# Expert rows of a mixture layer: weighted before they are stored, and gathered with an add into the residual

## The reference, cut to what matters

```
x = x + L0_attn(layernorm(x)); x = x + L0_xattn(layernorm(x), ctx)
x = x + L0_ffn(layernorm(x))     # 8 experts, 2 of them per token
x = x + L1_attn(layernorm(x))    # time mix (a scan over 256 tokens), then channel mix
x = x + L1_xattn(layernorm(x), ctx, bias); x = x + L1_ffn(layernorm(x))

# L0_ffn
probs = softmax(xt @ gate_w.T); top_w, top_i = top_k(probs, 2)
top_w = top_w / (sum(top_w) + 1e-9)
h   = gelu(xt @ w1[e] + b1[e]);  out_all = h @ w2[e] + b2[e]
out = sum_k top_w[k] * out_all[top_i[k]]
```

## Time and profile before

| | |
|---|---|
| median of 3 runs | 2008.58 us (2007.64 to 2011.26) |
| the profiled execution | 2000.81 us, its span 1999.0 us |
| PE busy | 1697.9 us, 85% of the span |
| DVE busy | 1245.6 us, 62% |
| ACT busy | 1120.9 us, 56% |
| POOL busy | 561.1 us, 28% |
| mean granted TensorE clock | 0.947 |

### The profile page before, as it was taken

The page is one execution under the profiler, slowest core; times in us unless marked ns, Lnnn a source line. Parts: engine busy times, 40 slices in busy tenths (PEclk is TensorE's granted clock), DMA queues, the critical chain, the costliest instruction groups (busy, mean ns, idle before and its releaser), DMA issues. The chain is left out here.

```text
span 1999.0 us, 40906 instructions
## 1 busy us (share of the span) xinstructions
PE 1697.9 (85%) x13535; PEld 1402.2 (70%) x13540; DVE 1245.6 (62%) x4276; ACT 1120.9 (56%) x2552; POOL 561.1 (28%) x719
## 2 busy tenths in 40 slices
PE   6677777774899999999956999999978999999963
PEld 5455555553688888889945777777866888888842
DVE  6689999868211111111118999998837988888756
ACT  2399999930222222223325666666627888888855
POOL 3333232330211111101025666666520000000017
PEclk9899999987899999999977999999999999999985
DMA  3100000025455555548930000000010000000002
GB/s 116 46 26 22 22 25 18 2 78 183 137 178 192 176 193 175 195 163 280 324 114 18 15 20 22 22 22 22 11 40 12 23 23 23 23 23 23 2 1 85
DMA packets 102048, 154.67 MB, mean 77 GB/s; under 512 B 5760, under 2 KB 85504, under 8 KB 101088
## 3 DMA queue, kind: packets, MB, share of 16 engines
q1 hardware_dynamic: 85600, 125.25, 19.1%
q0 software_dynamic: 6480, 17.70, 3.0%
q10 hardware_dynamic: 9776, 9.31, 1.3%
HBM read 134.54 MB, written 17.69 MB: 76 GB/s over the span
## 5 line engine op out<-in xcount | busy, mean ns | idle before, releaser
L1870 ACT ACTIVATE moe_hT<-moe_p_h,lane_a 128x256 f32<-128x256 f32 (+1 forms) x344 | 131.3, 433 | 370.1 <-PE moe_p_h L1822 370.1
L1822 PE MATMUL moe_p_h<-moe_gT,moe_w 128*128 128x256 f32 (+1 forms) x1376 | 255.8, 344 | 0.8 <-issue 0.8
L1832 PE MATMUL moe_p_y<-moe_w,moe_hT 128*128 128x256 f32 x1136 | 252.3, 379 | 0.0
L1822 PEld LDWEIGHTS moe_p_h<-moe_gT,moe_w 128*128 128x128 f32 x1376 | 227.4, 192 | 25.6 <-issue 1.2
L1362 ACT ACTIVATE xb_pr<-xb_sc,xb_nmax 128x256 f32<-128x256 f32 x512 | 225.3, 502 | 16.7 <-DVE xb_nmax L1441 16.5
L1832 PEld LDWEIGHTS moe_p_y<-moe_w,moe_hT 128*128 128x128 f32 x1136 | 212.6, 190 | 27.0
L1441 DVE CUSTOM_DVE_ANT_0 xb_sc<-xb_p_s,xb_neg 128x256 f32<-128x256 f32 x512 | 187.0, 419 | 55.1 <-PE xb_p_s L1204 46.2
L852 ACT ACTIVATE xa_pr<-xa_sc,xa_nmax 128x256 f32<-128x256 f32 (+1 forms) x512 | 204.6, 456 | 3.4 <-DVE xa_nmax L934 2.9
L1739 POOL DMA_INDIRECT moe_gx<-moe_tokens,moe_source_i x71 | 67.3, 947 | 456.5 <-PE moe_p_t L1809 400.4
L1990 DVE COPY moe_gT<-moe_p_t 128x512 f32<-128x512 f32 (+1 forms) x43 | 25.7, 598 | 232.0 <-PE moe_p_t L1809 232.0
L2015 DVE TENSOR_TENSOR moe_gy<-moe_p_y,lane_a 128x256 f32<-128x256 f32 x71 | 27.5, 420 | 229.1 <-PE moe_p_y L1832 229.1
(11 more groups left out here) (337 smaller groups left out, 3429.7 us busy)
## 6 DMA issues: line engine op xcount, KB each, us to landing
moe_w<-in_L_ffn_w_dram SPq DMA_DIRECT2D x86, 1024.0 KB, 8.1
moe_rows_out<-moe_gy ACTq DMA_DIRECT2D x28, 256.0 KB, 7.1
X<-in_x_dram SPq DMA_DIRECT2D x4, 1024.0 KB, 9.6
xa_ctx<-in_ctx_dram SPq DMA_DIRECT2D x16, 256.0 KB, 2.9
...
```

What stands on the lines that cost most here:

```text
L1822: last = pe.matmul(p_h[n % 3][:, k * width:(k + 1) * width], w1[:, r, ic, (2 * n + k) * P:(2 * n + k + 1) * P], gT[:, r % 2, ic, 0:width], ...
L1832: last = pe.matmul(p_y[:, t * D:(t + 1) * D], hT[:, hc, t * P:(t + 1) * P], w2[:, r, hc, :], start=(hc == 0), stop=(hc == HC - 1))
L1870: last = act.activation(hT[:, 2 * n + k, 0:width], p_h[n % 3][:, k * width:(k + 1) * width], ACT.Gelu, bias=b1[:, bass.ds(e * HC + 2 * n + ...
```

## The change

Three things change. (1) DVE works out `wt` before it waits for `counted`, and ACT's queue stores the 8192 weights, four bytes each, to a new array `weights` in memory. Token numbers in the table are shifted so that none is zero, and the one-hot products of the first and the second choice go to separate columns of `p_y`; from both DVE makes `source_i` as before and `weight_i`, the place of each slot's weight in `weights`. (2) POOL gathers each slot's weight behind the token rows of its group (71 more indirect gathers, of 128 single floats), DVE scales `b2` by it into `b2_w`, and `gy` becomes `p_y * weight + b2_w`, so that the rows in `rows_out` are weighted. (3) In the mix phase `which`, `got` and `combine` are gone: POOL gathers from `rows_out` straight into `X` with an add done by the DMA, indexed by `place_i`. The first choices of batch b + 5 and the second choices of batch b + 4 are issued in turn b; a second choice waits until the first choice of the same batch has landed. `measure_x(n)` waits for the second choice of batch n.

```diff
 # moe, POOL: token numbers without zero
+            chain.done(pool.tensor_scalar(token_up[:, :], token[:, :], 0.0, None, ALU.is_ge))
+            chain.wait()
+            chain.done(pool.tensor_tensor(token[:, :], token[:, :], token_up[:, :], ALU.add))
+            chain.wait()
...
+            def draw_weights(j):
+                if j >= RING:
+                    pool.wait_ge(s_["gy_ready"], j - RING + 1)
+                for t in range(tiles(j)):
+                    n = first_row(j) // P + t
+                    pool.indirect_dma_start(weight[:, j % RING, t:t + 1], None, weights,
+                                            bass.IndirectOffsetOnAxis(ap=weight_i[:, n:n + 1], axis=0)).then_inc(weighed[j % RING], 16)
...
+                if j == RING - 1:
+                    pool.wait_ge(s_["places_ready"], 1)
+                    pool.wait_ge(s_["loaded_back"], 16)
+                    for i in range(RING):
+                        draw_weights(i)
+                elif j >= RING:
+                    draw_weights(j)
 # moe, PE: one-hot products by choice
-                    last = pe.matmul(p_y[:, 0:NBLK], at_row[:, g % 4, n, :], at_blk[:, g % 4, n, :],
-                                     start=(g == 0 and n == 0), stop=(8 * g + n == 2 * NT - 1))
+                    k, at = divmod(8 * g + n, NT)
+                    last = pe.matmul(p_y[:, k * NBLK:(k + 1) * NBLK], at_row[:, g % 4, n, :], at_blk[:, g % 4, n, :],
+                                     start=(at == 0), stop=(at == NT - 1))
 # moe, ACT
+            act.wait_ge(s_["weights_ready"], 1)
+                act.dma_start(weights.rearrange("(k t p) a -> p (k t a)", k=2, p=P), wt[:, :, :].rearrange("p k t -> p (k t)")).then_inc(s_["loaded_back"], 16)
 # moe, DVE: behind gap_ready, ahead of counted (the same eight steps are taken out behind read_rows(0, 0))
+            dve.wait_ge(s_["exp_ready"], 1)
+            step(dve.tensor_reduce(zsum[:, :], probs[:, :, :], AX.X, ALU.add))
...
+            dve.sem_inc(s_["weights_ready"], 1)
 # moe, DVE: the inverse tables
-            dve.tensor_scalar(source_i[:, :], p_y[:, 0:NBLK], float(MID), None, ALU.add).then_inc(s_["source_ready"], 1)
+            step(dve.tensor_copy(codes[:, :, :], p_y[:, 0:2 * NBLK].rearrange("p (k n) -> p k n", k=2)))
+            step(dve.tensor_tensor(code[:, :], codes[:, 0, :], codes[:, 1, :], ALU.add))
+            step(dve.tensor_scalar(code_up[:, :], code[:, :], 0.0, -1.0, ALU.is_gt, ALU.mult))
+            step(dve.scalar_tensor_tensor(source[:, :], code[:, :], float(MID), code_up[:, :], ALU.add, ALU.add))
+            dve.tensor_copy(source_i[:, :], source[:, :]).then_inc(s_["source_ready"], 1)
+            step(dve.tensor_scalar(code_up[:, :], codes[:, 1, :], 0.0, float(B * S), ALU.not_equal, ALU.mult))
+            dve.tensor_tensor(weight_i[:, :], source[:, :], code_up[:, :], ALU.add).then_inc(s_["places_ready"], 1)
 # moe, DVE: per group
+                dve.wait_ge(weighed[r], drawn_by(j, r, i))
+                for t in range(tiles(j)):
+                    last = dve.tensor_scalar(b2_w[:, r % 2, t, :], b2[:, bass.ds(e, 1), :].rearrange("p a d -> p (a d)"), weight[:, r, t:t + 1], None, ALU.mult)
...
-                    last = dve.tensor_tensor(gy[:, r % 2, t, :], p_y[:, t * D:(t + 1) * D], b2[:, bass.ds(e, 1), :].rearrange("p a d -> p (a d)"), ALU.add)
+                    last = dve.scalar_tensor_tensor(gy[:, r % 2, t, :], p_y[:, t * D:(t + 1) * D], weight[:, r, t:t + 1], b2_w[:, r % 2, t, :], ALU.mult, ALU.add)
 # mix, POOL
-            def fetch(n, s):
-
-                if since(n, 2):
-                    wait_alone(pool, s_["stood_p"], (s_["combined"], n - 1))
-                pool.tensor_copy(which[:, s, :, :], place_i[:, :, bass.ds(TB * n, TB)]).then_inc(s_["which_ready"], 1)
-                wait_alone(pool, s_["stood_p"], (s_["which_ready"], n + 1))
-                for k in range(2):
-                    for t in range(TB):
-                        pool.indirect_dma_start(got[:, s, k, t, :], None, rows_out,
-                                                bass.IndirectOffsetOnAxis(ap=which[:, s, k, t:t + 1], axis=0)).then_inc(fetched[s], 16)
+            def fetch(n, k):
+
+                if k == 1:
+                    pool.wait_ge(fetched[0][n % 2], 32 * (n // 2) + 32)
+                for t in range(TB):
+                    pool.indirect_dma_start(tile_of(X, n, t), None, rows_out,
+                                            bass.IndirectOffsetOnAxis(ap=place_i[:, k, TB * n + t:TB * n + t + 1], axis=0),
+                                            compute_op=ALU.add).then_inc(fetched[k][n % 2], 16)
 
             fetch(0, 0)
-            fetch(1, 1)
+            fetch(1, 0)
...
+            fetch(0, 1)
+            fetch(1, 1)
             roots_x(0)
             change(0)
             fetch(2, 0)
+            fetch(3, 0)
+            fetch(2, 1)
+            fetch(4, 0)
+            fetch(3, 1)
             weigh(0)
...
-                if has_next(b, 3):
-                    fetch(b + 3, 1 - s)
+                if has_next(b, 5):
+                    fetch(b + 5, 0)
+                if has_next(b, 4):
+                    fetch(b + 4, 1)
 # mix, DVE: combine() and its calls are taken out, and
             def measure_x(n):
+                dve.wait_ge(fetched[1][n % 2], 32 * (n // 2) + 32)
```

More of the change, by code:

```diff
@@ L1575, in experts_ffn @@
     tokens = nc.dram_tensor("moe_tokens", (B * S, D), F32, kind="Internal").ap()
+    weights = nc.dram_tensor("moe_weights", (2 * B * S, 1), F32, kind="Internal").ap()
     with Phase(nc, "moe") as ph:
@@ L1623, in experts_ffn @@
         place = ph.sb("place", [P, 2, NT])
+        token_up = ph.sb("token_up", [P, NT])
+        codes = ph.sb("codes", [P, 2, NBLK])
+        code = ph.sb("code", [P, NBLK])
+        code_up = ph.sb("code_up", [P, NBLK])
+        source = ph.sb("source", [P, NBLK])
+        weight_i = ph.sb("weight_i", [P, NBLK], U32)
+        weight = ph.sb("weight", [P, RING, 2])
+        b2_w = ph.sb("b2_w", [P, 2, 2, D])
         blk = ph.sb("blk", [P, 2, NT])
@@ L1643, in experts_ffn @@
         names = ("warm_set set_up measured var_eps rstd_ready normed turned_x xT_ready logits lg_read "
-                 "gap_ready exp_ready both_ready counted owned hot hot_read source_ready gT_turned gT_ready hidden gelu_ready y_ready gy_ready "
+                 "places_ready weights_ready loaded_back bias_ready gap_ready exp_ready both_ready counted owned hot hot_read source_ready gT_turned gT_ready hidden gelu_ready y_ready gy_ready "
                  "chain_v chain_p stood_p").split()
@@ L1649, in experts_ffn @@
         drawn = [ph.sem(f"loaded_gx{i}") for i in range(RING)]
+        weighed = [ph.sem(f"loaded_gw{i}") for i in range(RING)]
         kept = [ph.sem(f"kept{i}") for i in range(2)]
@@ L1854, in _ @@
             act.activation(gap[:, :], gap[:, :], ACT.Exp).then_inc(s_["exp_ready"], 1)
+            act.wait_ge(s_["weights_ready"], 1)
+            with nc.allow_non_contiguous_dma(reason="one weight per token and choice"):
+                act.dma_start(weights.rearrange("(k t p) a -> p (k t a)", k=2, p=P), wt[:, :, :].rearrange("p k t -> p (k t)")).then_inc(s_["loaded_back"], 16)
             act.wait_ge(s_["owned"], 1)
@@ L1935, in _ @@
             dve.sem_inc(s_["gap_ready"], 1)
+            dve.wait_ge(s_["exp_ready"], 1)
+            step(dve.tensor_reduce(zsum[:, :], probs[:, :, :], AX.X, ALU.add))
+            step(dve.reciprocal(wt[:, 0, :], zsum[:, :]))
+            step(dve.tensor_tensor(wt[:, 1, :], gap[:, :], wt[:, 0, :], ALU.mult))
+            step(dve.tensor_tensor(wsum[:, :], wt[:, 0, :], wt[:, 1, :], ALU.add))
+            step(dve.tensor_scalar(wsum[:, :], wsum[:, :], 1e-9, None, ALU.add))
+            step(dve.reciprocal(wsum[:, :], wsum[:, :]))
+            for k in range(2):
+                chain.done(dve.tensor_tensor(wt[:, k, :], wt[:, k, :], wsum[:, :], ALU.mult))
+            chain.wait()
+            dve.sem_inc(s_["weights_ready"], 1)
             dve.wait_ge(s_["counted"], 1)
@@ L2059, in time_channel_mix @@
         Y = ph.sb("Y", [P, NT, D])
-        which = ph.sb("which", [P, 2, 2, TB], U32)
-        got = ph.sb("got", [P, 2, 2, TB, D])
         yn = ph.sb("yn", [P, TB, D])
@@ L2099, in time_channel_mix @@
                  "out_ready att_ready x_ready turned_m xc_ready mixed2_ready r2_ready th2_ready hidden relu_ready squared kv_ready g_ready "
-                 "with_y added which_ready combined chain_v chain_p stood_v stood_p stood_a").split()
+                 "with_y added chain_v chain_p stood_v stood_p stood_a").split()
         s_ = {n: ph.sem(n) for n in names}
-        fetched = [ph.sem(f"loaded_got{s}") for s in range(2)]
+        fetched = [[ph.sem(f"loaded_x{k}{s}") for s in range(2)] for k in range(2)]
         block = ph.block()
@@ L2447, in mix @@
                 last.then_inc(done, 1)
-            def combine(n, s, h):
-                dve.wait_ge(fetched[s], 64 * h + 64)
```

(10 more changed lines are left out.)

19 lines of the change are left out of this document (6 added, 13 removed).

## The result

| | before | after |
|---|---|---|
| median | 2008.51 us (2005.91 to 2015.55, 6 runs) | 2023.20 us (2022.73 to 2026.6, 6 runs) |
| profiled execution: span / time | 1999.0 / 2000.81 us | 2024.8 / 2026.6 us |
| ratio after / before | | 1.0067, 95% interval 1.0052 to 1.0081 |

The changed kernel is slower by 0.67% (10 to 16 us by the interval); the medians differ by 14.7 us. The two profiled executions differ by 25.8 us; 4.2 of that lie ahead of the tables and 3.4 behind the loop, in phases whose code is the same. Ahead of the tables PE's granted clock rose some 8 us later in this execution, and in the experiments the last `moe_gap` step started anywhere from 470.8 to 479.3 us. I therefore compare stage by stage, each from its own first row.

A forecast was written before the change was run, and what follows sets the result against it. PE was taken to bound the moe groups, with PE and DVE nearly level in the mix loop. Terms +2.7 + 0.5 + 1.0 + 1.6 - 9.5 = -3.7 us gave 2004.9 us from 2008.6; the range was 2000 to 2016.

The forecast's parts named there:

- the head of the mix phase: Start of the mix phase: statistics of batch 0 later (+1.0 us) and mix_gain_v's step (+1.6 us), together +2.6 us.
- the groups: Moe groups: 71 weight gathers double POOL's 13 us in 100, DVE scales b2 before its wait for PE; 0 us.
- Tables: Ahead of the groups: the weights' operations delay moe_total by 1.7 us, four more source_i steps add 1.0; +2.7 us.
- Scattered store: Weights stored as 8192 four-byte runs: from no cost to +3.2 us through late first token gathers; taken as +0.5 us.
- my 5.4 us: Estimate of the scattered weight store from the skill's 10.5 ns a packet, by which its term would be 0.
- the 1.6 us that I had named as a sign of being wrong: Gathers on POOL spaced above 1.6 us would prove the prediction wrong at that step; 1.25 us was expected.
- Loop: Mix loop: without combine, 2.97 us a turn leave DVE and the 13 turns get 9.5 us shorter.
- The adding gather is dearer to issue: Rival, chance 0.18: adding gathers cost POOL up to twice 1.26 us; 2012.5 us at half the upper bound, 2020 at it.
- The slow store: Rival, chance 0.10: weight packets above about 54 ns make the first gy wait; 2008 us at 48 ns, 2020 at 100.

The follow-up runs named there:

- e8_plain: The changed kernel with the mix phase's gathers overwriting X instead of adding to it; 2011.54 us, 1.0008 of the kernel before.
- e4_head: The changed kernel with four gathers instead of ten ahead of weigh(0), the other six behind change(1); 2016.28 us, 1.0039 of the kernel before.
- e2_mix_only: The moe phase of the kernel before with the mix phase of the changed kernel, weights of the choices left out; 2013.29 us, 1.0016 of the kernel before.

## Why the prediction was wrong

By the traces the forecast missed 21.9 us (+18.2 for -3.7), and two terms carry most of it: the head of the mix phase, +13.4 for +2.6, priced by a plain gather, and the groups, +8.3 for 0, by a mechanism that the forecast didn't have.

- **Tables, +2.7.** Right: A grew by 2.9 us. `moe_total` comes 3.17 us behind `moe_gap` (1.38 before), +1.8 for a forecast of +1.7; `moe_source_i` +1.1 for +1.0.
- **Scattered store, +0.5.** The mechanism was right, the size wrong. Of my two bounds, 0 and 48 ns a packet, I took one near 0, "because a packet of four bytes is nearer to none than to 1 KB". The mean record is 49 ns, and B grew by 2.9 us where the upper bound said 3.2. The Trainium skill's rule against a non-contiguous last dimension (*DMA: Bandwidth & Descriptors*, § Rules for kernel authors) holds here, 8208 packets. Its 10.5 ns a packet (§ Measured) is 0.67 us for the 64 packets of a whole load that GpSimd issues; I put it on the 512 packets of one engine, which the section doesn't say, and my 5.4 us is no estimate of this store, whose issue to landing took 28.2 us.
- **In the groups, 0.** This is the step whose mechanism failed, with 8.3 us. "POOL's 71 weight gathers double 13 us in 100" counts POOL's busy time and finds it free. It doesn't look at how the gathers stand: ten in a row became 18. While such a row lasts, the others see some of PE's increments late, and group 1 waits. No rival had this. Behind group 0 the zero was right: 496.73 us against 496.70.
- **Head of the mix phase, +2.6.** The term with the largest miss: right in mechanism and wrong by size, 13.4 us in D. The two steps I named are the ones that grew: the statistics of batch 0 (`mix_scale_x` 19.6 us behind the phase's start instead of 15.3, +4.3 for +1.0), and `mix_gain_v` against `mix_dif` (+8.3 for +2.4). The term rested on 1.26 us for a gather, the price of a plain one; an adding one took 1.85, above the 1.6 us that I had named as a sign of being wrong. At the plain price, in e8_plain, the two steps are -0.9 and +2.7 us, and D +0.4. The remaining 0.8 us of D weren't followed up; D moved by as much without an edit.
- **Loop, -9.5.** Right: -9.3, and the four dearer gathers a turn are hidden behind POOL's slack, as the rival's working said for half its upper bound.
- **The rivals.** Two of them came true at once. *The adding gather is dearer to issue* had the price almost exactly, 0.63 us at half its bound for a measured 0.60 (by luck: nothing but the halving of a bound stood behind it), but 7.6 us for the head where e8_plain shows 13.0. The ten gathers came as counted (+5.6 us against e8_plain); ahead of them two second choices were counted, 1.2 us, and the statistics of batch 0 came 5.2 us later, since four first choices and two longer landings stand there as well. In its favour I had written that the add needs the old value too, and then gave it 0.18. The Trainium skill's statement (*Collectives: The Full Stack*, § The bandwidth ceiling), that the two source reads slow the DMA, was read as sparing POOL; here both grew (POOL's 1.85 us for 1.25, its wait for the landing 4.3 for 3.1). *The slow store* was put to decide above 54 ns; what came is its case of 48 ns, +3.2 us, for a measured 2.9.

The terms by the traces: 2.9 + 2.9 + 8.3 + 13.4 - 9.3 = 18.2 us, against 14.7 in the medians (10 to 16). What remains is within what single executions differ by: e4_head's C is 6 us below the changed kernel's with the same code, and e2_mix_only, whose moe phase is that of before, has 0.5 us more in A and 0.3 in C than the kernel before.
